# Aggregation products over 128 neighbours, split into two products over 64 in separate PSUM banks

## The reference

```python
# x: (8, 2048, 512), adj: (2048, 2048) of 0 and 1, W: (512, 1024), b: (512,)
Wi, Wj = W[:, :512], W[:, 512:]
mi = einsum('bkd,od->bko', x, Wi)
mj = einsum('bkd,od->bko', x, Wj)
deg = adj.sum(axis=1)
out = deg[None, :, None] * (mi + b) + einsum('ij,bjo->bio', adj, mj)
return layernorm(x + out, eps=1e-5)
```

## Time and profile before

| | |
|---|---|
| median of 3 runs | 1672.72 us (1672.58 to 1673.87) |
| the profiled execution | 1672.83 us |
| its span, first to last instruction | 1670.8 us |
| PE busy | 1642.1 us (98%) |
| PE weight loads busy | 1354.5 us (81%) |
| DVE busy | 841.9 us (50%) |
| ACT busy | 667.4 us (40%) |
| POOL busy | 504.7 us (30%) |
| mean granted TensorE clock | 0.996 of 2.4 GHz |

### The profile page before, as it was taken

One profiled execution on the slowest core, in us unless ns is written; L12 is line 12 of the kernel. 1 busy time (PEld: TensorE's weight loads), 2 busy tenths in 40 slices (PEclk: granted clock), 3 DMA queues, 4 the chain that ended last, 5 costly groups with the idle time before them and its releaser, 6 DMA issues.

```text
span 1670.8 us, 24989 instructions
## 1 busy us (share of the span) xinstructions
PE 1642.1 (98%) x7248; PEld 1354.5 (81%) x7248; DVE 841.9 (50%) x1884; ACT 667.4 (40%) x970; POOL 504.7 (30%) x390
## 2 busy tenths in 40 slices
PE   7999999999999999999999999999999999999998
PEld 5878888788887888878888788887888878888786
DVE  7767754455444444445544444444454445444444
ACT  5665435423354323542345332453225433254321
POOL 2541124311343113431134311443114421144211
PEclk8999999999999999999999999999999999999999
DMA  5666522333223332343322332224322333232432
GB/s 171 192 185 214 184 82 91 123 110 104 81 95 119 113 107 75 100 126 105 97 86 95 123 109 94 91 92 132 107 88 88 100 126 107 82 101 82 126 111 71
DMA packets 102698, 187.26 MB, mean 112 GB/s; under 512 B 11408, under 2 KB 11408, under 8 KB 102672
## 3 DMA queue, kind: packets, MB, share of 16 engines
q1 hardware_dynamic: 84528, 153.92, 29.0%
q10 hardware_dynamic: 18144, 33.04, 6.5%
HBM read 119.80 MB, written 67.11 MB: 112 GB/s over the span
## 4 chain that ended last, share of the span: by engine, by line
PE 96%; ACT 1%; DVE 1%; issue 1%; DMA 0%; ACTq 0%; SPq 0%; DVEq 0%
PE agg_ps L329 56%; PE cross_ps L295 14%; PE main_ps L305 13%; PE main_ps L307 13%; ACT adjT L411 1%; DVE W_lo L478 0%; DMA mi_dram<-mi 0%; ACT mj_hi L399 0%; PE deg_ps L314 0%; DMA mi_in<-in_wt 0%; DVE deg_part L523 0%; DVE W_df L480 0%; DVE mj L475 0%; DVE cross L475 0%; ACT cross L395 0%
## 5 line engine op out<-in xcount | busy, mean ns | idle before, releaser
L329 PE MATMUL agg_ps<-mj_hi,adjT 128*128 128x512 f32 x2048 | 798.0, 390 | 10.6 <-ACT adjT L411 9.3
L329 PE MATMUL agg_ps<-mj_lo,adjT 128*128 128x512 f32 x2048 | 796.9, 389 | 0.0
L411 ACT ACTIVATE adjT<-adjT 128x2048 fp32r (+1 forms) x128 | 244.4, 1916 | 548.4 <-PE agg_ps L329 548.4
L329 PEld LDWEIGHTS agg_ps<-mj_hi,adjT 128*128 128x128 f32 x2048 | 384.5, 188 | 93.5 <-POOL mj_lo L252 10.1
L329 PEld LDWEIGHTS agg_ps<-mj_lo,adjT 128*128 128x128 f32 x2048 | 384.4, 188 | 79.6
L305 PE MATMUL main_ps<-W_hi,x_hi 128*128 128x512 f32 x1024 | 399.4, 390 | 0.3 <-DVE mi L509 0.3
L307 PE MATMUL main_ps<-W_lo,x_lo 128*128 128x512 f32 x1024 | 398.9, 390 | 0.0
L258 POOL TENSOR_TENSOR mi_in<-mi_in,bias 128x512 f32<-128x512 f32 x128 | 166.0, 1299 | 664.3 <-DMA mi_in<-mi_dram 664.3
L295 PE MATMUL cross_ps<-W_df,x_df 128*128 128x512 f32 x1024 | 276.4, 392 | 10.0 <-POOL x_df L247 7.7
L252 POOL TENSOR_TENSOR mj_lo<-mj,mj_hi 128x512 f32 (+1 forms) x128 | 173.0, 1351 | 293.5 <-ACT mj_hi L399 293.5
L543 DVE TENSOR_TENSOR r<-agg_ps,r 128x512 f32<-128x512 f32 x128 | 88.5, 692 | 336.2 <-PE agg_ps L329 336.0
(11 more groups left out here) (43 smaller groups left out, 577.5 us busy)
## 6 DMA issues: line engine op xcount, KB each, us to landing
mi_dram<-mi SPq DMA_DIRECT2D x128, 256.0 KB, 2.0
mi_in<-mi_dram SPq DMA_DIRECT2D x128, 256.0 KB, 2.7
r<-in_x SPq DMA_DIRECT2D x128, 256.0 KB, 2.7
out<-r SPq DMA_DIRECT2D x128, 256.0 KB, 2.0
x_raw<-in_xt ACTq DMA_DIRECT2D x126, 256.0 KB, 2.7
adj_in<-in_adjt SPq DMA_DIRECT2D x64, 256.0 KB, 3.1
r<-in_wt SPq DMA_DIRECT2D x4, 256.0 KB, 5.4
x_raw<-in_xt SPq DMA_DIRECT2D x2, 256.0 KB, 3.8
```

The lines of the kernel that those rows point to most:

```text
L329: last = nc.tensor.matmul(agg_ps[s][:, :], adjT[s][:, j, :], part[:, j, :], start=(j == 0 and part is mj_hi), stop=(j == NT - 1 and part i ...
L411: nc.scalar.activation(adjT[s][:, :, :], adjT8[:, :, bass.ds(i * P, P)], ACT.Copy).then_inc(adjT_ready, 1)
```

## The change

Each product of an aggregation becomes two: one of SBUF partitions 0 to 63 (rows 0 to 63 of the array), one of partitions 64 to 127 (rows 64 to 127). Both have 128 output rows and 512 columns. The lower half accumulates in the bank `agg_ps[s][0]`, the upper in `agg_ps[s][1]`, and they alternate product by product. With two tiles in turn that takes four banks. DVE adds the two banks one after the other, with a semaphore `half_ready` between the adds, and raises `sum_ready` after the second.

Since no bank is left for the degrees, `degrees(0)` writes to `agg_ps[1][1]`, and the three others to `main_ps[0]`, which is free during the aggregation; PE waits for the last `mj` and for the degrees taken before.

```diff
-        agg_ps = [pb(f"agg_ps{s}") for s in range(2)]
-        deg_ps = pb("deg_ps")
+        agg_ps = [[pb(f"agg_ps{s}{q}") for q in range(2)] for s in range(2)]
+        deg_ps = [agg_ps[1][1], main_ps[0], main_ps[0], main_ps[0]]
...
             def degrees(q):
                 pe.wait_ge(deg_part_ready, NT * (q + 1))
+                if q:
+                    pe.wait_ge(mj_ready, NT)
+                    pe.wait_ge(deg_ready, q)
                 for t in range(TPB):
-                    last = nc.tensor.matmul(deg_ps[:, 2 * t:2 * t + 2], deg_part[:, t * P:(t + 1) * P], ones[:, :],
+                    last = nc.tensor.matmul(deg_ps[q][:, 2 * t:2 * t + 2], deg_part[:, t * P:(t + 1) * P], ones[:, :],
...
                     for part in (mj_hi, mj_lo):
-                        last = nc.tensor.matmul(agg_ps[s][:, :], adjT[s][:, j, :], part[:, j, :],
-                                                start=(j == 0 and part is mj_hi),
-                                                stop=(j == NT - 1 and part is mj_lo))
+                        for q in range(2):
+                            last = nc.tensor.matmul(agg_ps[s][q][:, :], adjT[s][64 * q:64 * q + 64, j, :],
+                                                    part[64 * q:64 * q + 64, j, :],
+                                                    start=(j == 0 and part is mj_hi),
+                                                    stop=(j == NT - 1 and part is mj_lo))
...
                 if zero:
+                    pe.wait_ge(deg_ready, 1)
                     for i in range(NT):
...
                 dve.wait_ge(agg_done, m + 1)
-                nc.vector.tensor_tensor(r[u][:, :], agg_ps[s][:, :], r[u][:, :], ALU.add).then_inc(sum_ready, 1)
+                nc.vector.tensor_tensor(r[u][:, :], agg_ps[s][0][:, :], r[u][:, :], ALU.add).then_inc(half_ready, 1)
+                dve.wait_ge(half_ready, m + 1)
+                nc.vector.tensor_tensor(r[u][:, :], agg_ps[s][1][:, :], r[u][:, :], ALU.add).then_inc(sum_ready, 1)
```

More of the change, by code:

```diff
@@ L120, in bass_adj_resnorm @@
         agg_done = sem("agg_done")
+        half_ready = sem("half_ready")
         sum_ready = sem("sum_ready")
@@ L366, in _ @@
                 for _ in range(4):
-                    nc.tensor.matmul(agg_ps[0][:, 0:P], warm[:, :], warm[:, :], start=True, stop=True)
+                    nc.tensor.matmul(agg_ps[0][0][:, 0:P], warm[:, :], warm[:, :], start=True, stop=True)
             over_batches(pe, batch)
@@ L528, in take_degrees @@
                 nc.vector.tensor_copy(deg[:, q * TPB:(q + 1) * TPB],
-                                      deg_ps[:, 0:2 * TPB].rearrange("p (t c) -> p t c", c=2)[:, :, 0]
+                                      deg_ps[q][:, 0:2 * TPB].rearrange("p (t c) -> p t c", c=2)[:, :, 0]
                                       ).then_inc(deg_ready, 1)
```

## The result

| | before | changed kernel |
|---|---|---|
| median of the runs | 1672.65 us (1671.66 to 1673.87) | 1681.35 us (1679.82 to 1682.42) |
| ratio | | 1.0048, 95% interval 1.0036 to 1.0061 |
| profiled execution | 1672.83 us, span 1670.8 | 1682.42 us, span 1680.6 |

A forecast was written before the change was run, and what follows sets the result against it. PE bounds, through the 226.95 ns between aggregation products. Pairs add 0, the first batch 2.5, other mode changes 2.4, the end 0.8: 5.7 us on 1672.8 makes 1678.5 us, range 1658 to 1728.

The forecast's parts named there:

- Streaming: Aggregation on PE: both halves stream together, so a pair keeps the 226.95 ns of one whole-array product; cost 0 us.
- a paid extra in each pair: Rival, aggregation: each pair costs 3 to 12 ns extra, giving 1691 to 1728 us; chance 0.20.
- a bare load: Rival, aggregation: one weight load in each pair is not hidden, pace 338 ns, 2135 us; chance 0.05.
- no overlap: Rival, aggregation: the halves run one after the other, 930 us more, 2608 us; chance 0.16.
- Loads: Aggregation: two weight loads per pair at 111.4 ns take 222.8 ns, 4 ns under the pace, so barely hidden.
- The sign that was to be seen, loads 111 ns apart: Expected in the profile: the aggregation's weight loads nearly back to back, 111 ns apart.
- The rival built on it, 1661.7 us: Rival, aggregation: loads set the pace at 222.8 ns, 17 us go, 1661.7 us; chance 0.22.
- Changes of mode: PE between whole array and halves: 0.27 us each, nine counted at returns to projection and around degree products, 2.4 us.
- First batch: DVE's second add does not fit there: last chunk and `degrees(3)` move to 195.4 us, PE 2.5 us later.
- the prediction's own sign of being wrong: Aggregation stages: a granted clock other than 1.00 inside them would make all of the prediction wrong.
- The end: After the last product DVE's chain is bare, so the second add costs 0.8 us.
- In batches 1 to 7 it fits: DVE's second add, 0.78 us a tile, fits in its idle time in batches 1 to 7; cost 0.

The follow-up runs named there:

- e4: The changed kernel with four products over 32 rows each, four banks and four adds, each tile waiting for the adds of the one before: 2355.24 us.
- e6: The changed kernel with ACT's split of x for the next batch's second tile ahead of the last root: 1678.68 us, ratio 1.0030.
- f2: The changed kernel with the split of x ahead of the last root and the first two adjacency tiles widened within the projection: 1668.15 us, ratio 0.9970.
- e2: The kernel before, whole-array products and one bank, with a second DVE add of the same bank: 1681.09 us, ratio 1.0049.
- e1: The changed kernel without DVE's second add, so the upper halves' sum is left out: 1674.58 us, ratio 1.0009.
- e7: The changed kernel with two products of the lower half, then two of the upper, in turn: 1684.08 us in one run.
- e8: The changed kernel with four products of the lower half, then four of the upper, in turn: 1686.28 us in one run.
- e5: The changed kernel with later adjacency chunks cast and counted earlier and the third degree product ahead of tile 6, not 7: 1681.12 us, ratio 1.0051.
- e9: The changed kernel with eight products of the lower half, then eight of the upper, in turn: 1835.92 us in one run.
- e3: The changed kernel with all 32 products of the lower half first, then the 32 of the upper: 3685.92 us in one run.
- e10: The changed kernel with sixteen products of the lower half, then sixteen of the upper, in turn: 3167.01 us in one run.
- f1: The kernel before with the split of x ahead of the last root and the first two adjacency tiles of batches 1 to 7 widened within the projection: 1660.81 us.

## Why the prediction was right, and where its sum was off

Forecast and direction held: 1678.5 us said, 1681.35 measured, and the mechanism named for the products is the one that the trace shows. That the time came so near is in part luck: more than half of the loss stands where the sum had 0. Term by term:

- *Streaming, "226.95 ns, cost 0".* Right: 226.7 ns a pair, 116.38 us a stage. The rivals of a paid extra in each pair, of a bare load and of no overlap fall with it. The 4 ns that the Trainium skill gives for each further tile (TensorE: Matmul & The Clock Gate, Part 3, Packing small matmuls) are not paid by a stream of pairs: 4096 x 4 ns would be 16 us, and the stages grew by 0.02. The second product of a pair does start a little behind the first, by 3 to 4 ns at 119 us and by 10 ns at 400 us.
- *Loads, "222.8 ns, hidden, but barely".* Wrong in its working. 111.4 ns is the distance of loads into the same rows; loads into different rows run side by side (10 ns apart in the changed kernel, four in 227 ns in e4). The sign that was to be seen, loads 111 ns apart, is not there. The rival built on it, 1661.7 us, had no basis.
- *Changes of mode, 0.27 us each, 9 of them 2.4 us.* Too dear: out of the halves and back again costs 0.26 us around degree products (1.30 against 1.04), 0.13 a change, and a bare change at a stage's end 0.2 us (a distance of 0.32 and one of 0.34 in place of two of 0.23; that is the gap that was to be seen at each return). Of the nine only the one behind `degrees(3)` came on top of the waits, 0.2 us; the seven returns to projection were hidden behind the wait for `x_df` and are bare in e6 and f2. That there is a price at all agrees with what the Trainium skill says of a drain (TensorEngine Tiling (Array Packing), Key Properties).
- *First batch, `degrees(3)` at 195.4 us.* Right: 195.26 (2.35 us later than before, 0.24 of it from the start), with PE idle for 1.47 us and `deg_part` as the releaser; 1.4 was said. What the sum did not have is the stretch at half clock behind it, 1.6 us. A clock other than 1.00 inside a stage was the prediction's own sign of being wrong; here it lasted 3.4 us.
- *The end, 0.8 us.* Right: 0.75.
- *"In batches 1 to 7 it fits", cost 0.* **This step failed.** I read the mean, 5.83 of 10 us busy, and the adds inside a pass, and did not follow the last add of a batch to who waits for it. That add is on a chain of DVE, ACT, POOL and PE, which already ended at PE in the kernel before. It costs 0.7 us at each of seven batch ends, 4.9 us, more than half of the loss. e2 makes it without the halves, e1 and e6 take it away.

By the spans: 5.7 us said, less 0.4 at `degrees(3)` and 2.2 of mode changes, plus 1.6 of clock, 4.9 of batch ends and 0.2 of the start, make 9.8, as measured between the two profiled executions. The errors had opposite signs, so the forecast was nearer than its working deserved.

Left open: what brings the half clock after the wait at `degrees(3)` and how often. Six profiles have a wait of about 1.5 us there, and in five of them the dip follows (changed kernel, e6, e7, e8 and f2, not e2); the three with a short wait or none (e1, e5, e9) have no dip. Of the changed kernel's four timed executions the fastest, 1679.82 us, has a mean granted clock of 0.996 and the others, from 1681.14 us, 0.995, which is the size of one such dip; but a dip at the start-up would look the same. Open too: why one or two stages of e3 and e10 ran at full clock and the rest didn't; and whether a semaphore set by the last product of one half always covers the other half, now that the two can run out of order, above all where the last product stands within four of a swap, as in e7 and e8. The last was not tried.

## What to carry to other kernels

Splitting a contraction that already fills the array gives PE nothing: two halves at once take the time of the whole, and the sum has to be made elsewhere. Before an operation on a half-idle engine is costed at nothing, follow the last one of each stage through every queue to the engine that bounds; the mean busy share speaks of the middle of a stage, and the price is paid at its ends. And look at that chain first: mending ACT's order there and at the start of a stage gained 12 us (f1), more than the 8.7 that the change lost.

## What the runs showed of the hardware that I had not expected

- Products of the two halves of the array need not alternate in the program: at each swap of the half the first four of the new half run beside the last four of the old, which wins 0.75 to 0.77 us at full clock, from blocks of 8 to blocks of 32 (e9, e10, e3), and about 1.5 us at half clock (e3, e10). Alternating, in twos or in fours, the pace is full (116.4 to 116.6 us a stage).
- Weight loads into different rows run side by side: four in 227 ns (e4), against 111.4 ns each into the same rows.
- The granted clock was 0.50 in most stages of e3 and e10, with PE busy 10 of 10 us on products over 64 rows, of which a quarter (e3) and half (e10) had a partner by the count of four at each swap; in e9, where all have one, it was 1.00 from the first aggregation to the last. Why is not shown.
